# Layer norm at the end of a graph kernel: scaled sum and input joined on VectorE, deviation by square root and reciprocal

## The chip, the cores and the metric

The kernel runs on one core of a Trainium2 chip. The time is the device time of that core in microseconds (us), the median of several executions. A profile is one execution taken by the hardware profiler. It has its own time, and within that a span, from the first instruction to the last.

## The reference, cut to what matters

A graph layer computes a message for each of 200000 edges, sums the messages into 12500 nodes of 64 features (`agg`), and then normalises in two steps:

```
new_node = g3 * (agg - mean0(agg)) * rsqrt(var0(agg) + 1e-5) + bt3      # per feature, over all nodes
h        = x + (x + new_node)
out      = (h - mean(h)) / sqrt(var(h) + 1e-5)                          # per node, over its 64 features
```

The change touches only these last lines: the batch norm's scale and shift, the sum with `x` taken twice, and the layer norm over 64 features.

## The kernel before, in words

Features lie on partitions and nodes on columns. A tile of 128 partitions holds two halves of the nodes, 64 features each, so all of it is 128 x 6250. The last stage cuts that into `PARTS`: N = 13 parts, twelve of 500 columns and one of 250. Everything before it (the edge stages, some 2487 us of the span) is left as it is.

The order of the work is written out by hand, one program per engine, with semaphores between them. A wait is on a count, so that slot n % 4 of a buffer (S = 4) or n % 3 (V = 3) is used again only when part n - 4 or n - 3 is done with it.

First half of the stage. TensorE folds `agg` into `y_ps` (L983), VectorE takes the statistics of each part (`bn_stats`, L1040), and ScalarE copies it to `total` (L1012). Then comes a serial stretch of tiny instructions, `norm_coefficients` (L1067 on) with two products in `pair_sums`. It gives scale and shift of each feature in `bn3`. One of its instructions is a reciprocal of one column (L1091). Its root runs on ScalarE (L1014).

Between the halves, VectorE scales the 128 x 128 centring matrix by the feature's scale (`centre_t`, L1044). TensorE makes the centred shift (L992), and VectorE copies it to `shift` (L1046). GpSimd has built the block average `average`, `centre` = identity minus average, and `centre_x` = 2 * centre.

Second half, for each part n:

- TensorE puts `centre_x` times x and `centre_t` times total into one `y_ps` (L1001, L1002), and behind that `average` times the square of part n - 1 into `var_ps` (L997).
- ScalarE squares `y_ps` with the shift as bias (L1031), and makes the inverse deviation of part n - 1 by Ln (L1024) and Exp with scale -0.5 (L1026).
- GpSimd squares the inverse deviation (L972), VectorE multiplies by the variance (L1052), makes y by a multiplication with the inverse deviation (L1053), and turns the product into the factor of a Newton step (L1056). GpSimd multiplies y by it (L966).
- SyncE sends y to memory, one DMA a part (L947), when GpSimd is done with it.

GpSimd's order is: square of part n, then the last multiplication of part n - 1.

Of the kernel before, what the change touches and what calls it, by code (L numbers as in the profile page):

```python
# [17 lines left out]
P = 128  # L18
# [89 lines left out]
def build(nc, xt, x_nodes, src_t, src_r, dst_t, dst_r, dst_h, dst_hr, e_main, e_ragged,  # L108
          x, w_dst, w_src, w_edges, b1, g1, bt1, g2, bt2, g3, bt3, out):
    ctx = ExitStack()  # L110
    with ctx:
# [15 lines left out]
        def sem(name):  # L127
            return ctx.enter_context(nc.semaphore(name))
# [35 lines left out]
        with stage:  # L164
            def sb(name, shape, dt=F32):
                return stage.enter_context(nc.sbuf_tensor(name, shape, dt))
# [736 lines left out]
        with stage:  # L903
            def sb(name, shape, dt=F32):
# [7 lines left out]
            x_sb = sb("x_sb", [P, N_HALF])  # L912
            total = sb("total", [P, N_HALF])
            square = [sb(f"square{s}", [P, COLS]) for s in range(S)]
            inv_dev = [sb(f"inv_dev{s}", [P, COLS]) for s in range(S)]
            refine = [sb(f"refine{s}", [P, COLS]) for s in range(V)]
            eps = sb("eps", [P, 1])
            y = sb("y", [P, N_HALF])
            average = sb("average", [P, P])
            centre = sb("centre", [P, P])  # L920
            centre_x = sb("centre_x", [P, P])
            centre_t = sb("centre_t", [P, P])
            stats = sb("stats3", [P, N, 6])
            shift = sb("shift", [P, 1])
            y_ps = [stage.enter_context(nc.psum_tensor(f"y_ps{s}", [P, 512], F32)) for s in range(S)]
# [4 lines left out]
                sem(n) for n in ("x_in4", "folded", "f_copied", "f_counted", "aggr3", "paired3", "rooted3", "bn3_steps"))  # L930
            averages, centres, scaled, shift_summed, shift_set = (
                sem(n) for n in ("averages", "centres", "scaled", "shift_summed", "shift_set"))
            centred, squared, averaged, logged, inverted, inv_squared, multiplied, divided, refined, normed, stored = (
                sem(n) for n in ("centred", "squared", "averaged", "logged3", "inverted", "inv_squared", "multiplied",
                                 "divided", "refined", "normed", "stored"))

            def width(n):
                return PARTS[n].stop - PARTS[n].start
# [3 lines left out]
            @blk.sync  # L942
            def _(sp):
                sp.dma_start(x_sb[:], x_nodes).then_inc(x_in4, 16)
                for n in range(N):
                    sp.wait_ge(normed, n + 1)
                    sp.dma_start(out[:, PARTS[n]], y[:, PARTS[n]]).then_inc(stored, 16)  # L947
                sp.wait_ge(stored, 16 * N)

            @blk.gpsimd  # L950
            def _(gp):
                gp.memset(eps[:], EPS).then_inc(averages, 1)
                gp.memset(average[:], 0.0).then_inc(averages, 1)
                gp.wait_ge(averages, 2)
                for h in range(2):
                    lanes = slice(h * F, (h + 1) * F)
                    gp.memset(average[lanes, lanes], 1.0 / F).then_inc(averages, 1)
                gp.wait_ge(averages, 4)
                gp.tensor_tensor(centre[:], ident[:], average[:], ALU.subtract).then_inc(centres, 1)
                gp.wait_ge(centres, 1)  # L960
                gp.tensor_tensor(centre_x[:], centre[:], centre[:], ALU.add).then_inc(centres, 1)

                def finish(n):
                    gp.wait_ge(divided, n + 1)
                    gp.wait_ge(refined, n + 1)
                    gp.tensor_tensor(y[:, PARTS[n]], y[:, PARTS[n]], refine[n % V][:, 0:width(n)], ALU.mult).then_inc(normed, 1)  # L966

                for n in range(N):
                    part = inv_dev[n % S][:, 0:width(n)]
                    gp.wait_ge(inverted, n + 1)  # L970
                    after(gp, normed, n - V + 1)
                    gp.tensor_tensor(refine[n % V][:, 0:width(n)], part, part, ALU.mult).then_inc(inv_squared, 1)  # L972
                    if n > 0:
                        finish(n - 1)
                finish(N - 1)

            @blk.tensor
            def _(pe):
                for n in range(N):
                    after(pe, f_counted, n - S + 1)  # L980
                    after(pe, f_copied, n - S + 1)
                    for h in range(2):
                        mm = pe.matmul(y_ps[n % S][h * F:(h + 1) * F, 0:width(n)], fold[:, 0:F],  # L983
                                       agg[:, h * N_HALF + PARTS[n].start:h * N_HALF + PARTS[n].stop], start=True, stop=True)
                    mm.then_inc(folded, 1)
                pair_sums(pe, fold, tmp, pair_ps, aggr, paired)
                pe.wait_ge(x_in4, 16)
                pe.wait_ge(f_copied, N)
                pe.wait_ge(averages, 4)
                pe.wait_ge(centres, 2)  # L990
                pe.wait_ge(scaled, 1)
                pe.matmul(pair_ps[:, 2:3], centre[:], bn3[:, 1:2], start=True, stop=True).then_inc(shift_summed, 1)  # L992

                def variance(n):
                    pe.wait_ge(squared, n + 1)
                    after(pe, multiplied, n - V + 1)
                    pe.matmul(var_ps[n % V][:, 0:width(n)], average[:], square[n % S][:, 0:width(n)], start=True, stop=True).then_inc(averaged, 1)  # L997

                for n in range(N):
                    after(pe, divided, n - S + 1)  # L1000
                    pe.matmul(y_ps[n % S][:, 0:width(n)], centre_x[:], x_sb[:, PARTS[n]], start=True, stop=False)  # L1001
                    pe.matmul(y_ps[n % S][:, 0:width(n)], centre_t[:], total[:, PARTS[n]], start=False, stop=True).then_inc(centred, 1)  # L1002
                    if n > 0:
                        variance(n - 1)
                variance(N - 1)

            @blk.scalar
            def _(act):
                for n in range(N):
                    act.wait_ge(folded, n + 1)  # L1010
                    act.wait_ge(f_counted, n + 1)
                    act.activation(total[:, PARTS[n]], y_ps[n % S][:, 0:width(n)], ACT.Copy).then_inc(f_copied, 1)  # L1012
                act.wait_ge(aggr, 3)
                act.activation(tmp[:, 7:8], tmp[:, 6:7], ACT.Sqrt).then_inc(rooted, 1)  # L1014
                act.preload_act_table_set("natural_log_exp_and_others")
                act.wait_ge(averages, 4)
                act.wait_ge(shift_set, 1)

                def invert(n):

                    part = inv_dev[n % S][:, 0:width(n)]
                    act.wait_ge(averaged, n + 1)
                    after(act, divided, n - S + 1)
                    act.activation(part, var_ps[n % V][:, 0:width(n)], ACT.Ln, bias=eps[:]).then_inc(logged, 1)  # L1024
                    act.wait_ge(logged, n + 1)
                    act.activation(part, part, ACT.Exp, scale=-0.5).then_inc(inverted, 1)  # L1026

                for n in range(N):
                    act.wait_ge(centred, n + 1)
                    after(act, averaged, n - S + 1)  # L1030
                    act.activation(square[n % S][:, 0:width(n)], y_ps[n % S][:, 0:width(n)], ACT.Square, bias=shift[:]).then_inc(squared, 1)  # L1031
                    if n > 0:
                        invert(n - 1)
                invert(N - 1)

            @blk.vector
            def _(v):
                for n in range(N):
                    v.wait_ge(folded, n + 1)
                    v.bn_stats(stats[:, n, :], y_ps[n % S][:, 0:width(n)]).then_inc(f_counted, 1)  # L1040
                norm_coefficients(v, stats[:], f_counted, N, gb[:, 4:5], gb[:, 5:6], bn3,
                                  tmp, pair_ps, aggr, paired, rooted, bn3_steps)
                v.wait_ge(centres, 1)
                v.tensor_scalar(centre_t[:], centre[:], bn3[:, 0:1], None, ALU.mult).then_inc(scaled, 1)  # L1044
                v.wait_ge(shift_summed, 1)
                v.tensor_copy(shift[:], pair_ps[:, 2:3]).then_inc(shift_set, 1)  # L1046
                v.wait_ge(shift_set, 1)

                for n in range(N):
                    part = refine[n % V][:, 0:width(n)]  # L1050
                    v.wait_ge(inv_squared, n + 1)
                    v.scalar_tensor_tensor(part, var_ps[n % V][:, 0:width(n)], eps[:], part, ALU.add, ALU.mult).then_inc(multiplied, 1)  # L1052
                    v.scalar_tensor_tensor(y[:, PARTS[n]], y_ps[n % S][:, 0:width(n)], shift[:], inv_dev[n % S][:, 0:width(n)],  # L1053
                                           ALU.add, ALU.mult).then_inc(divided, 1)
                    v.wait_ge(multiplied, n + 1)
                    v.tensor_scalar(part, part, -0.5, 1.5, ALU.mult, ALU.add).then_inc(refined, 1)  # L1056


def pair_sums(pe, fold, tmp, pair, aggr, paired):
# [87 lines left out]
```

## Time and profile before

| what | us |
|---|---|
| median of 3 runs (2549.99 to 2551.42) | 2550.4 |
| the profiled execution's own time | 2551.55 |
| its span | 2549.6 |
| first half of the last stage and its coefficients, in the span | from 2487.4 |
| second half | from about 2506 |

The page's row of engines gives busy time over the whole span, most of which belongs to the edge stages. The stage of the change is the last fortieth of it, so the rows below are read from stretches of the trace near its end. Instants are microseconds from the span's start.

### The profile page before, as it was taken

What the parts mean: (1) busy time and instruction counts of PE and PEld (TensorE: products, weight loads), DVE (VectorE), ACT (ScalarE), POOL (GpSimd) and SP (SyncE); (2) the same over time, 40 slices, a digit from 0 to 9 for tenths busy, and PEclk for the clock granted to TensorE, in tenths of its full rate; (3) what the DMA queues carried; (4) which work ended last, traced back from release to release, by engine and by line L of the source; (5) the groups of instructions that cost most, each with busy time, mean ns of one, the idle gap of its engine ahead of it and who ended that gap; (6) DMA issues with size and microseconds to landing.
All of it is one profiled execution on the core that took longest, in us unless ns stands there. A gap on an engine that the chain in (4) does not pass through costs nothing. (4 is left out here: it accounts for less than half of the span.)

```text
span 2549.6 us, 31587 instructions
## 1 busy us (share of the span) xinstructions
PE 1829.1 (72%) x7288; PEld 775.3 (30%) x7288; DVE 1008.4 (40%) x1958; ACT 688.7 (27%) x724; POOL 1745.7 (68%) x1679
## 2 busy tenths in 40 slices
PE   5987778777878777787777787877777005776667
PEld 3322222222222222222222222222222004665553
DVE  4322222222222222222222222222223897887785
ACT  0111111111111111111111111111111978998835
POOL 7777777777777777777777777777775106666624
PEclk7766666666666666666666666666666558999998
DMA  7433333333333333333333333333345895876522
GB/s 210 118 92 99 92 98 91 93 97 90 97 94 90 101 91 95 96 90 98 93 92 99 90 94 97 94 96 91 94 126 192 302 353 198 257 248 215 190 83 101
DMA packets 247313, 327.52 MB, mean 128 GB/s; under 512 B 78146, under 2 KB 130762, under 8 KB 246957
## 3 DMA queue, kind: packets, MB, share of 16 engines
q1 hardware_dynamic: 167961, 220.98, 26.6%
q0 software_dynamic: 50048, 51.30, 10.4%
q10 hardware_dynamic: 29232, 54.42, 5.8%
q8 instruction: 27, 0.44, 0.1%
q14 instruction: 45, 0.37, 0.0%
HBM read 234.57 MB, written 91.96 MB: 128 GB/s over the span
## 5 line engine op out<-in xcount | busy, mean ns | idle before, releaser
L331 POOL DMA_INDIRECT rows<-x,idx x1564 | 1478.5, 945 | 480.6 <-issue 475.6
L536 DVE BATCH_NORM_STATS2 stats<-z_sb 128x512 f32 (+1 forms) x196 | 135.7, 692 | 1004.6 <-ACT z_sb L431 1004.6
L376 PE MATMUL xg_ps<-ident,rows 128*128 128x128 f32 (+1 forms) x782 | 213.5, 427 | 417.0 <-DMA rows<-x,idx 416.9
L370 PE MATMUL d_ps<-d_two,ones 1*84 1x512 f32 (+1 forms) x784 | 403.8, 636 | 11.3 <-DMA d_two<-dst_f 11.3
L380 PE MATMUL z_ps<-e_in,w_edge 96*128 96x512 f32 x392 | 373.3, 1056 | 0.0
L425 ACT ACTIVATE xg<-xg_ps 128x512 f32<-128x512 f32 x196 | 116.7, 596 | 899.8 <-PE xg_ps L376 899.8
L389 PE MATMUL z_ps<-xg,w_rows 128*128 128x512 f32 x392 | 346.0, 983 | 0.2 <-ACT xg L425 0.2
L431 ACT ACTIVATE z_sb<-z_ps 128x512 f32<-128x512 f32 x196 | 116.7, 596 | 799.7 <-PE z_ps L384 799.7
L376 PEld LDWEIGHTS xg_ps<-ident,rows 128*128 128x128 f32 (+1 forms) x782 | 136.2, 212 | 595.9 <-DMA rows<-x,idx 428.5
L759 POOL TENSOR_TENSOR h_buf<-h_buf,s_all 128x1536 f32<-128x1536 f32 x66 | 223.4, 3417 | 110.0 <-ACT h_buf L733 110.0
L519 DVE TENSOR_SCALAR hot<-d_ps,node_col 84x512 f32<-84x512 f32 x392 | 274.5, 740 | 41.2 <-PE d_ps L370 30.6
L384 PE MATMUL z_ps<-hot,q_in 84*64 84x512 f32 (+1 forms) x784 | 278.9, 799 | 0.5 <-DVE hot L519 0.5
L770 PE MATMUL sum_ps<-near,h_rows 128*64 128x84 f32 x3128 | 158.7, 244 | 97.4 <-DVE agg L822 90.6
L370 PEld LDWEIGHTS d_ps<-d_two,ones 1*84 1x84 f32 x784 | 105.6, 154 | 344.0 <-issue 332.5
L389 PEld LDWEIGHTS z_ps<-xg,w_rows 128*128 128x128 f32 x392 | 123.9, 316 | 209.5 <-ACT xg L425 111.6
L450 DVE COPY idx<-src_idx 128x8 int32 (+1 forms) x195 | 35.3, 182 | 364.0 <-PE xg_ps L376 358.1
L770 PEld LDWEIGHTS sum_ps<-near,h_rows 128*64 128x64 f32 x3128 | 131.2, 139 | 128.1 <-issue 103.8
L830 DVE COPY h_rows<-turn_ps 128x512 f32<-128x512 f32 x196 | 129.3, 687 | 17.3 <-PE turn_ps L780 7.0
L384 PEld LDWEIGHTS z_ps<-hot,q_in 84*64 84x64 f32 x784 | 49.9, 176 | 266.2 <-issue 266.2
L629 DVE BATCH_NORM_STATS2 stats<-s_all 128x512 f32 (+1 forms) x195 | 116.9, 677 | 6.0 <-ACT s_all L612 5.4
L822 DVE TENSOR_TENSOR agg<-agg,sum_ps 64x84 f32 x392 | 93.4, 238 | 51.7 <-issue 42.9
L745 ACT ACTIVATE h_buf<-s_all,bn 128x1536 f32<-128x1536 f32 x66 | 108.3, 1641 | 20.0 <-PE turn_ps L780 19.7
(122 smaller groups left out, 1056.8 us busy)
## 6 DMA issues: line engine op xcount, KB each, us to landing
s_all<-edge_mem SPq DMA_DIRECT2D x118, 768.0 KB, 6.5
edge_mem<-z_sb ACTq DMA_DIRECT2D x195, 256.0 KB, 2.1
e_in<-e_main SPq DMA_DIRECT2D x195, 192.0 KB
near_mem<-near_one SPq DMA_DIRECT2D x195, 168.0 KB, 2.0
near<-near_mem SPq DMA_DIRECT2D x65, 504.0 KB, 3.8
rows<-x,idx POOLq DMA_INDIRECT x1564, 2.5
q_in<-q_table SPq DMA_DIRECT2D x392, 21.0 KB
agg<-xt SPq DMA_DIRECT2D x7, 448.0 KB, 10.7
```

The source lines that it names most:

```text
L331: gp.indirect_dma_start(out=rows[s][0:size.tile, t, h, :], out_offset=None, in_=x, in_offset=bass.IndirectOffsetOnAxis(ap=idx[s][0:size.ti ...
L370: mm = pe.matmul(d_ps[0:WIN, h, 0:w], ones[s % 2 * F:s % 2 * F + 1, 0:WIN], d_in[s][:, h, 0:w], start=True, stop=True)
L376: mm = pe.transpose(xg_ps[s % 2][:, t * size.tile:(t + 1) * size.tile], rows[s][0:size.tile, t, :, :].rearrange("p h f -> p (h f)"), ident ...
L380: pe.matmul(z_ps[s % 2][:, 0:w], w_edge[:], e_in[s][:, 0:w], start=True, stop=False)
L384: mm = pe.matmul(z_ps[s % 2][h * F:(h + 1) * F, 0:w], which(h), hot[:, h, 0:w], start=False, stop=last)
L389: pe.matmul(z_ps[s % 2][:, 0:w], w_rows[:], xg[s % 2][:, 0:w], start=False, stop=False)
L519: hots = v.tensor_scalar(hot[:, h, 0:size.half], d_ps[0:WIN, h, 0:size.half], node_col[0:WIN, bass.ds(g * 2 + h, 1)], None, ALU.is_equal)
L536: v.bn_stats(stats[:, bass.ds(g, 1), :].rearrange("p a k -> p (a k)"), z_sb[s][:, 0:size.half]).then_inc(z_counted, 1)
L629: ins = v.bn_stats(stats[:, bass.ds(c * CHUNK + k, 1), :].rearrange("p a k -> p (a k)"), s_in[s][:, k, :])
L759: gp.tensor_tensor(m.cols(h_buf[m.slot % H]), m.cols(h_buf[m.slot % H]), m.cols(s_in[m.slot]), ALU.mult).then_inc(h_ready, 1)
L770: mm = pe.matmul(sum_ps[k][h * F:(h + 1) * F, 0:WIN], h_rows[m.slot % 2][0:n.tile, k, t, h * F:(h + 1) * F], hots[0:n.tile, h * n.tiles + ...
L830: v.tensor_copy(h_rows[m.slot % 2][:, k][at], turn_of(m, k)[at]).then_inc(rows_ready, 1)
```

## The change

The two products into `y_ps` become one. VectorE now joins each part beforehand: total = total * (scale / 2) + x (`join`). Everything is thus at half the size of before, and the epsilon is a quarter to match. `centre_t` and `centre_x` are gone. The shift is halved in the instruction that took it out of PSUM.

The deviation is a square root on ScalarE, then a `reciprocal` on VectorE over the whole part, in place. Ln, Exp, GpSimd's square, the two VectorE instructions of the Newton step and GpSimd's multiplication are gone. GpSimd has nothing left to do in the second half. The table of the square root is loaded at the start of the stage and stays. The output DMA waits for VectorE.

VectorE's order: join of parts 0, 1, 2, then for each n: reciprocal of n, join of n + 3, y of n. All waits on `x` are VectorE's now.

```diff
-                gp.memset(eps[:], EPS).then_inc(averages, 1)
+                gp.memset(eps[:], EPS / 4).then_inc(averages, 1)
...
-                gp.wait_ge(centres, 1)
-                gp.tensor_tensor(centre_x[:], centre[:], centre[:], ALU.add).then_inc(centres, 1)
-
-                def finish(n):
-                    gp.wait_ge(divided, n + 1)
-                    gp.wait_ge(refined, n + 1)
-                    gp.tensor_tensor(y[:, PARTS[n]], y[:, PARTS[n]], refine[n % V][:, 0:width(n)], ALU.mult).then_inc(normed, 1)
-
-                for n in range(N):
-                    part = inv_dev[n % S][:, 0:width(n)]
-                    gp.wait_ge(inverted, n + 1)
-                    after(gp, normed, n - V + 1)
-                    gp.tensor_tensor(refine[n % V][:, 0:width(n)], part, part, ALU.mult).then_inc(inv_squared, 1)
-                    if n > 0:
-                        finish(n - 1)
-                finish(N - 1)
...
+                pe.wait_ge(f_copied, N)
                 for n in range(N):
+                    pe.wait_ge(joined, n + 1)
                     after(pe, divided, n - S + 1)
-                    pe.matmul(y_ps[n % S][:, 0:width(n)], centre_x[:], x_sb[:, PARTS[n]], start=True, stop=False)
-                    pe.matmul(y_ps[n % S][:, 0:width(n)], centre_t[:], total[:, PARTS[n]], start=False, stop=True).then_inc(centred, 1)
+                    pe.matmul(y_ps[n % S][:, 0:width(n)], centre[:], total[:, PARTS[n]], start=True, stop=True).then_inc(centred, 1)
...
             def _(act):
+                act.preload_act_table_set("sqrt_and_others")
...
-                act.preload_act_table_set("natural_log_exp_and_others")
...
-                def invert(n):
-
-                    part = inv_dev[n % S][:, 0:width(n)]
+                def deviation(n):
                     act.wait_ge(averaged, n + 1)
                     after(act, divided, n - S + 1)
-                    act.activation(part, var_ps[n % V][:, 0:width(n)], ACT.Ln, bias=eps[:]).then_inc(logged, 1)
-                    act.wait_ge(logged, n + 1)
-                    act.activation(part, part, ACT.Exp, scale=-0.5).then_inc(inverted, 1)
+                    act.activation(dev[n % S][:, 0:width(n)], var_ps[n % V][:, 0:width(n)], ACT.Sqrt, bias=eps[:]).then_inc(rooted_dev, 1)
...
-                v.wait_ge(centres, 1)
-                v.tensor_scalar(centre_t[:], centre[:], bn3[:, 0:1], None, ALU.mult).then_inc(scaled, 1)
+                v.tensor_scalar(half_scale[:], bn3[:, 0:1], 0.5, None, ALU.mult).then_inc(scaled, 1)
                 v.wait_ge(shift_summed, 1)
-                v.tensor_copy(shift[:], pair_ps[:, 2:3]).then_inc(shift_set, 1)
+                v.tensor_scalar(shift[:], pair_ps[:, 2:3], 0.5, None, ALU.mult).then_inc(shift_set, 1)
                 v.wait_ge(shift_set, 1)
-
+                v.wait_ge(scaled, 1)
+                v.wait_ge(x_in4, 16)
+
+                def join(n):
+
+
+                    v.wait_ge(f_copied, n + 1)
+                    v.scalar_tensor_tensor(total[:, PARTS[n]], total[:, PARTS[n]], half_scale[:], x_sb[:, PARTS[n]],
+                                           ALU.mult, ALU.add).then_inc(joined, 1)
+
+                for n in range(V):
+                    join(n)
                 for n in range(N):
-                    part = refine[n % V][:, 0:width(n)]
-                    v.wait_ge(inv_squared, n + 1)
-                    v.scalar_tensor_tensor(part, var_ps[n % V][:, 0:width(n)], eps[:], part, ALU.add, ALU.mult).then_inc(multiplied, 1)
-                    v.scalar_tensor_tensor(y[:, PARTS[n]], y_ps[n % S][:, 0:width(n)], shift[:], inv_dev[n % S][:, 0:width(n)],
-                                           ALU.add, ALU.mult).then_inc(divided, 1)
-                    v.wait_ge(multiplied, n + 1)
-                    v.tensor_scalar(part, part, -0.5, 1.5, ALU.mult, ALU.add).then_inc(refined, 1)
+                    v.wait_ge(rooted_dev, n + 1)
+                    part = dev[n % S][:, 0:width(n)]
+                    v.reciprocal(part, part).then_inc(inverted, 1)
+                    if n + V < N:
+                        join(n + V)
+                    v.wait_ge(inverted, n + 1)
+                    v.scalar_tensor_tensor(y[:, PARTS[n]], y_ps[n % S][:, 0:width(n)], shift[:], part, ALU.add, ALU.mult).then_inc(divided, 1)
```

## Rows read from the trace of the kernel before

**Rows 1.** The page: span, and engines' busy time over the whole span.
```profile
span 2549.6 us, 31587 instructions
PE 1829.1 (72%) x7288; PEld 775.3 (30%) x7288; DVE 1008.4 (40%) x1958; ACT 688.7 (27%) x724; POOL 1745.7 (68%) x1679
```

**Rows 2.** Busy time of each engine, coefficients, start, loop and tail of the stage.
```profile
core 0: us, PE busy (x) PEld busy (x) DVE busy (x) ACT busy (x) POOL busy (x), PEclk, DMA share, GB/s
2502.00:2506.00 4.00, 1.28 (x6) 1.14 (x6) 1.72 (x10) 2.84 (x4) 0.00 (x0) 0.63 0.00 0
2506.00:2511.00 5.00, 5.00 (x9) 2.32 (x9) 0.16 (x1) 0.68 (x1) 0.00 (x0) 0.61 0.01 2
2511.00:2547.20 36.20, 28.94 (x72) 13.22 (x70) 25.31 (x39) 24.14 (x38) 29.27 (x26) 0.96 0.21 80
```

**Rows 3.** Chain of waits, start and one loop turn: start, duration, engine, tile, line.
```profile
2508.13 1.67 PE y_ps L1002 x2
...
2522.86 1.24 POOL y L966
2524.09 1.17 POOL refine L972
2525.28 0.74 DVE refine L1052
2526.02 0.65 DVE y L1053
2526.67 1.08 DVE refine L1056
...
2527.89 1.24 POOL y L966
```

**Rows 4.** Groups by line and shape, 2470 to 2550: busy us, mean ns of one.
```profile
L966 POOL TENSOR_TENSOR y<-y,refine 128x500 f32<-128x500 f32 x12 | 14.9, 1245 | 2.1 <-DVE refine L1056 2.1
L997 PE MATMUL var_ps<-square,average 128*128 128x500 f32 x24 | 12.0, 582 | 0.0
L1053 DVE SCALAR_TENSOR_TENSOR y<-y_ps,shift,inv_dev 128x500 f32<-128x500 f32 x12 | 8.7, 727 | 0.0
L1053 DVE SCALAR_TENSOR_TENSOR y<-y_ps,shift,inv_dev 128x250 f32<-128x250 f32 x1 | 0.5, 469 | 0.0
L1031 ACT ACTIVATE square<-y_ps,shift 128x500 f32<-128x500 f32 x12 | 8.1, 677 | 8.7 <-PE y_ps L1002 8.7
L1024 ACT ACTIVATE inv_dev<-var_ps,eps 128x500 f32<-128x500 f32 x12 | 8.1, 677 | 1.8 <-PE var_ps L997 1.8
```

**Rows 5.** VectorE and TensorE in order of time, in the loop.
```profile
2518.97 1.00 PE L997 MATMUL var_ps<-square,average 128*128 128x500 f32 x2
2519.80 1.00 PE L1001 MATMUL y_ps<-x_sb,centre_x 128*128 128x500 f32 x2
2527.66 0.73 DVE L1052 SCALAR_TENSOR_TENSOR refine<-var_ps,eps,refine 128x500 f32<-128x500 f32 x1
2528.31 0.72 DVE L1053 SCALAR_TENSOR_TENSOR y<-y_ps,shift,inv_dev 128x500 f32<-128x500 f32 x1
2528.95 0.45 DVE L1056 TENSOR_SCALAR refine<-refine 128x500 f32<-128x500 f32 x1
```

**Rows 6.** Single lines of VectorE: count, duration ns min/median/max, first and last start.
```profile
L1091 DVE RECIPROCAL tmp<-tmp x3: 164/165/165, 1981.0 to 2504.5; 128x1 f32<-128x1 f32 x3
L1092 DVE TENSOR_TENSOR bn<-tmp,gb x3: 159/159/159, 1981.2 to 2504.7; 128x1 f32<-128x1 f32 x3
L641 DVE TENSOR_SCALAR high<-high x1: 153/153/153, 2114.3 to 2114.3; 128x1 f32<-128x1 f32 x1
L812 DVE TENSOR_TENSOR near<-iota_ps,rel x65: 1198/1208/1209, 2117.4 to 2473.1; 128x1008 f32<-128x1008 f32 x65
```

**Rows 7.** In order of time, from the coefficients into the loop, and the last instruction.
```profile
2505.26 0.28 DVE L1044 TENSOR_SCALAR centre_t<-centre,bn 128x128 f32<-128x128 f32 x1
2505.69 0.56 PE L992 MATMUL pair_ps<-bn,centre 128*128 128x1 f32 x2 [1.73 <-DVE centre_t L1044]
2506.29 0.16 DVE L1046 COPY shift<-pair_ps 128x1 f32<-128x1 f32 x1 [0.74 <-PE pair_ps L992]
...
2546.41 0.71 POOL L966 TENSOR_TENSOR y<-y,refine 128x250 f32<-128x250 f32 x1 [0.29 <-DVE refine L1056]
```

**Rows 8.** Table loads, the load of x, and the last copies to total.
```profile
L1014 ACT ACT_TABLE_LOAD x1 | 1.3, 1283 | 0.0
L1015 ACT ACT_TABLE_LOAD x1 | 1.3, 1283 | 0.0
x_sb<-x_nodes SPq DMA_DIRECT2D x1, 3125.0 KB, 10.6
2487.39 0.34 SPq L944 DMA_DIRECT2D x_sb<-x_nodes  x1
2501.21 0.86 ACT L1012 ACTIVATE total<-y_ps 128x500 f32<-128x500 f32 x2 [0.25 <-DVE stats L1040]
```

More of the change, by code:

```diff
@@ L914, in build @@
             square = [sb(f"square{s}", [P, COLS]) for s in range(S)]
-            inv_dev = [sb(f"inv_dev{s}", [P, COLS]) for s in range(S)]
-            refine = [sb(f"refine{s}", [P, COLS]) for s in range(V)]
+            dev = [sb(f"dev{s}", [P, COLS]) for s in range(S)]
             eps = sb("eps", [P, 1])
@@ L920, in build @@
             centre = sb("centre", [P, P])
-            centre_x = sb("centre_x", [P, P])
-            centre_t = sb("centre_t", [P, P])
+            half_scale = sb("half_scale", [P, 1])
             stats = sb("stats3", [P, N, 6])
@@ L932, in build @@
                 sem(n) for n in ("averages", "centres", "scaled", "shift_summed", "shift_set"))
-            centred, squared, averaged, logged, inverted, inv_squared, multiplied, divided, refined, normed, stored = (
-                sem(n) for n in ("centred", "squared", "averaged", "logged3", "inverted", "inv_squared", "multiplied",
-                                 "divided", "refined", "normed", "stored"))
+            joined, centred, squared, averaged, rooted_dev, inverted, divided, stored = (
+                sem(n) for n in ("joined", "centred", "squared", "averaged", "rooted_dev", "inverted", "divided", "stored"))
             def width(n):
@@ L945, in _ @@
                 for n in range(N):
-                    sp.wait_ge(normed, n + 1)
+                    sp.wait_ge(divided, n + 1)
                     sp.dma_start(out[:, PARTS[n]], y[:, PARTS[n]]).then_inc(stored, 16)
@@ L986, in _ @@
                 pair_sums(pe, fold, tmp, pair_ps, aggr, paired)
-                pe.wait_ge(x_in4, 16)
-                pe.wait_ge(f_copied, N)
                 pe.wait_ge(averages, 4)
-                pe.wait_ge(centres, 2)
+                pe.wait_ge(centres, 1)
                 pe.wait_ge(scaled, 1)
@@ L995, in variance @@
                     pe.wait_ge(squared, n + 1)
-                    after(pe, multiplied, n - V + 1)
+                    after(pe, rooted_dev, n - V + 1)
                     pe.matmul(var_ps[n % V][:, 0:width(n)], average[:], square[n % S][:, 0:width(n)], start=True, stop=True).then_inc(averaged, 1)
+                pe.wait_ge(f_copied, N)
                 for n in range(N):
+                    pe.wait_ge(joined, n + 1)
                     after(pe, divided, n - S + 1)
-                    pe.matmul(y_ps[n % S][:, 0:width(n)], centre_x[:], x_sb[:, PARTS[n]], start=True, stop=False)
-                    pe.matmul(y_ps[n % S][:, 0:width(n)], centre_t[:], total[:, PARTS[n]], start=False, stop=True).then_inc(centred, 1)
+                    pe.matmul(y_ps[n % S][:, 0:width(n)], centre[:], total[:, PARTS[n]], start=True, stop=True).then_inc(centred, 1)
                     if n > 0:
@@ L1032, in _ @@
                     if n > 0:
-                        invert(n - 1)
-                invert(N - 1)
+                        deviation(n - 1)
+                deviation(N - 1)
             @blk.vector
```

## The prediction
> **What bounds the kernel now.** I read the page first: GpSimd and TensorE are busy for 68% and 72% of 2549.6 us [rows 1], but that is the edge stages, which the diff leaves alone. So I read the end of the span by stretches [rows 2]. The coefficients (2502 to 2506) are serial, with every engine mostly idle. In the next 5 us TensorE works without a gap at a granted clock of 0.61. Then the loop takes 36.2 us at 0.96, with GpSimd busy for 29.27 of it and TensorE for 28.94. VectorE has 25.31 and ScalarE 24.14.
>
> The chain of waits [rows 3] shows one turn: 5.03 us (2522.86 to 2527.89) between GpSimd's multiplications two parts apart, so 2.51 us a part, through GpSimd and VectorE in turn. TensorE is level with it. It starts one fp32 product of 500 columns each 0.83 us (2518.97, 2519.80) [rows 5], and three a part are 2.5 us. So the loop has two limits at about 2.5 us, and a part needs both shortened.
>
> **The change part by part.**
>
> *Removed.* Each part loses two instructions of GpSimd (L972, L966), two of VectorE (L1052, L1056), Exp on ScalarE, and one of three products on TensorE. What was 2.5 us on TensorE becomes 2 x 0.84 = 1.68 us. ScalarE keeps two instructions of 677 ns [rows 4], 1.36 us; I take the root at Ln's price, since Ln and Square, with the same operands, cost the same 677 ns. GpSimd has nothing to do. By these alone the loop would run at about 1.7 us a part. What is late next is VectorE.
>
> *VectorE, a part.* Three instructions: reciprocal, join, y.
>
> - y is L1053 as before: 727 ns for 500 columns, 469 ns for 250 [rows 4], so 1.03 ns a column. In a row of instructions each starts 0.65 us after the one in front (2527.66, 2528.31) [rows 5], 0.08 less than its duration. I take 0.65.
> - The join has the same form, but both tensors in SBUF. The nearest two-tensor row is 1208 ns for 1008 columns [rows 6], and 159 ns for one column. So 159 + 500 x 1.04 = 0.68 us, 0.60 from start to start. Bounds: 0.60 and 0.74, the latter the L1052 row in the chain. They move the sum by about 1.3 us.
> - The reciprocal of 500 columns does not occur in this trace. Only one of a single column does: 164 to 165 ns, where a two-tensor instruction of one column takes 159 and a scalar one 153 [rows 6]. One element lengthens the instruction by 5 to 6 ns over its neighbour. If all elements went through in a stream as in other instructions, one element should cost what theirs does. I therefore read the surplus as a price that each element pays: 1.03 + 5 to 1.03 + 6, that is 6.03 to 7.03 ns a column. I take the middle, 6.53: 500 x 6.53 + 160 = 3.42 us, and 1.79 us for 250 columns. Low end: a fixed surplus and 1.03 ns a column (or the 0.45 us of the scalar instruction L1056 [rows 5]). High end: the surplus over L641, 12 ns, paid by every column: 13.03 ns, 6.7 us.
>
> The Trainium skill, "VectorE: DVE Perf Modes", section "First, the fixed hardware budget", speaks against this change. It says that reciprocal is an iterated divide with a repeat count of 8 on two of the eight slices. The one-column surplus agrees in kind. Taken as eight passes of 1.03 ns it is the second rival below.
>
> *The loop.* With a join, a turn is (3.42 - 0.08) + 0.60 + 0.65 = 4.59 us. Joins run for n = 0 to 9, the last of them of 250 columns (0.34). Then: nine turns of 4.59 = 41.31; one of 4.33; two without a join, 3.42 + 0.03 + 0.65 = 4.10 each, 8.20 (y now waits for the reciprocal, with nothing between); the last 1.79 + 0.03 + 0.47 = 2.29. Sum 56.1 us.
>
> Does anything starve VectorE? The product of part n + 3 needs join n + 3, and the variance of n + 2 is queued behind it on TensorE. The root needed at the start of turn n + 1 hangs on join n + 2, which ended in turn n - 1, over 4 us earlier. Behind it are two products (0.84 each), a square and a root (0.68 each): 3.0 us. Even at the lower clock, where one product took 1.67 us of the chain [rows 3], TensorE needs 3.4 us a part, below 4.59. So neither TensorE nor ScalarE is seen, and the gap that TensorE now has costs nothing.
>
> *The start.* The 128 x 128 scaling (0.28) becomes a one-column instruction (0.16), so L992 starts 0.12 earlier, at 2505.57, and the shift is there at 2506.35 [rows 7]. New in the path is join 0, 0.68 us, to 2507.05, where before TensorE went straight on to x. Then at the lower clock two products of 1.67 (0 and 1, to about 2510.5), the variance of 0 (0.84 to 1.67), the root 0.15 + 0.68. The first reciprocal starts at 2512.2 to 2513.0; I take 2512.6. The joins of 1 and 2 lie beside product 0.
>
> *The new waits.* The joins wait for x, which landed 10.6 us after its issue at 2487.4 [rows 8], about 2498, so it is not late. The copies to `total` end at 2502.1 [rows 8]. The SyncE queue waits for y rather than for GpSimd's multiplication, and 250 KB every 4.6 us is less than it moved before. The two table loads of 1.28 us [rows 8] were already beside other work: the first ran in the wait for the coefficients, the second beside VectorE's last of them. Costed at 0 either way; uncovered they would give 1.3 us each.
>
> *The tail.* Before, the last instruction ended at 2546.41 + 0.71 = 2547.12, and the span 2.48 us later [rows 1, 7]. The last DMA is the same, so I keep that.
>
> *Sum.* 2512.6 + 56.1 + 2.5 = 2571.2, against a span of 2549.6: +21.6 us. On the profiled execution's own time that is 2551.55 + 21.6 = 2573.2. The median of the runs stands 1.15 under this, so I predict 2572.
>
> All 6250 columns pay, so the result moves by 6.25 us for each ns in the price of a column: the difference is 21.6 + 6.25 x (price - 6.53). It is zero at 3.07 ns. At 6.03 it is +18.5, at 7.03 +24.7.
>
> **The rivals.**
>
> 1. *Faster: the reciprocal streams.* At 1.03 ns a column a turn of VectorE is 0.60 + 0.60 + 0.65 = 1.85 us, still above TensorE's 1.68, and the difference is 21.6 - 6.25 x 5.5 = -12.8: 2537.6. It decides below 3.07 ns, 1.7 us for 500 columns. For it: VectorE's other instructions all show near 1 ns a column or less, and the surplus of 6 ns may be the start of a longer pipe. Against: that surplus is nearly six times the price of a column, and it is the same in all three instances. 12%.
> 2. *Eight passes a column.* 8 x 1.03 = 8.24 ns, 4.28 us for 500 columns, +32.3: 2582.7. For it: a one-column row cannot tell well what part of the fixed time a reciprocal saves, as the 153 ns of L641 shows against 159. Against: eight passes would show 7.2 ns over the two-tensor row, where 5 to 6 are seen. 23%. At the far end, 13.03 ns, it would be 2612.6; 4%.
> 3. *The tables switch in the loop.* If Square did not lie in the root's set, two loads of 1.28 us a part would stand beside ScalarE's 1.36: 3.9 us a part. At my price it hides behind the 4.59 of VectorE, apart from one or two loads at the start, some 2.6 us: 2575. If the reciprocal streams, 13 x (3.9 - 1.85) would turn -12.8 into about +14: 2564. For it: the trace has no Sqrt of many columns, and Square was seen only behind the Ln table. 3%.
>
> The Trainium skill, "ScalarE: Activation LUTs", section "Table sets: the hidden batching unit", says that cheap functions lie in every set and that only the anchors switch. No row here shows Square under the root's table.
>
> **How the numbers follow.** Price of a column between 5.3 and 7.6 ns, the forecast: 58%, 2564 to 2579. Rival 1 12%, rival 2 and its far end 27%, rival 3 3%. The range 2565 to 2584 takes in eight passes and rival 3, and leaves out rival 1, the far end and the edges of the forecast. This kernel's measurement tells 0.2%, 5.1 us, from no change. Faster by more is rival 1 without prices between 2 and 4 ns: 11%. Within 0.2%: 2%. Slower: 87%.
>
> **What would show it.** The group of RECIPROCAL rows of 128x500: 3.4 us each, thirteen of them on the chain of waits, with VectorE busy without gaps from about 2512 to 2569, and TensorE and ScalarE waiting for it. y 0.73 and join 0.68 us. Two products of 0.84 us a part or, if the clock falls in TensorE's gaps, longer with no effect. No GpSimd and at most one table load in the stage. Reciprocal rows near 0.7 us would make the prediction wrong in sign, rows over 4 us in size; a chain that goes through TensorE or ScalarE in the loop would refute the step that nothing starves VectorE.

## The result, and the profile after

The changed kernel takes 2571.47 us (median of 4 runs, 2570.59 to 2572.41), the kernel before 2550.91 in the same comparison. The ratio is 1.0078, with a 95% interval of 1.0061 to 1.0096: slower by 20.6 us. The prediction said 2572, in a range of 2565 to 2584.

The edge stages are the same code in both, yet the profiled execution of after reached the last stage about 2 us later. So the parts are compared by the *stage*: from the start of the aggregation of the last statistics (2501.48 before, 2503.41 after) to the end of the span (2549.6, 2570.1). That is 48.1 us before and 66.7 after, +18.6. The other 1.9 us of the two spans lie ahead of the change, in code that both share. In the four kernels of the experiments that ran beside each other, the same code brought the stage's start anywhere from 2500.16 to 2503.03.

Busy time of each engine by stretch, after (columns as in [rows 2]), start and loop:

```profile
2506.00:2511.00 5.00, 2.38 (x5) 1.36 (x6) 3.08 (x10) 0.20 (x1) 0.00 (x0) 0.50 0.00 0
2511.00:2567.20 56.20, 30.81 (x51) 10.31 (x49) 53.06 (x35) 17.08 (x26) 0.00 (x0) 0.77 0.14 54
```

Against [rows 2], where four engines shared 36.2 us, VectorE alone is now busy for 53.06 of 56.2. GpSimd has nothing. TensorE's granted clock has fallen from 0.96 to 0.77, and its 30.81 us for two thirds of the products (28.94 us for all of them before) show the price, yet it ends far below VectorE.

The chain of waits after, from the first product to the end of one turn (start, duration, engine, tile, line), and the last turns. It answers to [rows 3]:

```profile
2508.29 0.75 DVE total L1030
...
2509.18 3.30 PE y_ps L982 x4
2512.48 0.85 PE var_ps L976 x2
...
2513.36 0.69 ACT dev L1002
...
2514.07 3.28 DVE dev L1038
2517.34 0.56 DVE total L1030
2517.90 0.65 DVE y L1042
2518.55 3.18 DVE dev L1038
...
2565.72 1.63 DVE dev L1038
```

In the loop the chain has only one engine. L1038 is the reciprocal, L1030 the join, L1042 y. The first turn is 2514.07 to 2518.55, and each is 4.39 us from there on. The groups by line and shape, which answer to [rows 4, 6]:

```profile
L1038 DVE RECIPROCAL dev<-dev 128x500 f32<-128x500 f32 x12 | 39.2, 3266 | 3.7 <-ACT dev L1002 3.7
L1038 DVE RECIPROCAL dev<-dev 128x250 f32<-128x250 f32 x1 | 1.7, 1707 | 0.0
L1042 DVE SCALAR_TENSOR_TENSOR y<-y_ps,shift,dev 128x500 f32<-128x500 f32 x12 | 8.8, 730 | 0.1
L1030 DVE SCALAR_TENSOR_TENSOR total<-total,half_scale,x_sb 128x500 f32<-128x500 f32 x12 | 7.8, 661 | 0.0
L982 PE MATMUL y_ps<-total,centre 128*128 128x500 f32 x24 | 17.3, 820 | 17.9 <-DVE total L1030 17.9
L1002 ACT ACTIVATE dev<-var_ps,eps 128x500 f32<-128x500 f32 x12 | 8.1, 677 | 6.5 <-PE var_ps L976 6.5
L989 ACT ACT_TABLE_LOAD x1 | 1.3, 1283 | 39.7 <-PEq L661 39.7
```

The two reciprocal shapes give (3266 - 1707) / 250 = 6.24 ns a column. The root costs what Ln did, 677 ns. One table load stands in the whole stage.

### The profile page after: what moved, and what is told of

It is laid out like the page before. It is cut to its first block and busy times, and to the rows that moved or that the text cites. A ratio compares the mean times of both kernels' runs of the same rounds, so it can differ in the third digit from the quotient of the medians.

```text
span 2570.1 us, 31480 instructions
## 1 busy us (share of the span) xinstructions
PE 1819.5 (71%) x7262; PEld 766.4 (30%) x7262; DVE 1038.5 (40%) x1958; ACT 679.6 (26%) x710; POOL 1717.4 (67%) x1652
## 5 line engine op out<-in xcount | busy, mean ns | idle before, releaser
L380 PE MATMUL z_ps<-e_in,w_edge 96*128 96x512 f32 x392 | 367.0, 1039 | 0.0
```

The lines of the kernel that those rows point to most:

```text
L380: pe.matmul(z_ps[s % 2][:, 0:w], w_edge[:], e_in[s][:, 0:w], start=True, stop=False)
```

## The experiments

There were ten runs, of nine kernels (e6 and e10 are the same one). Four shared one comparison, in which the kernel before took 2551.2 us. The other six ran in two comparisons, on two other chips, in which the kernel before itself took 3014 and 3034 us. There the edge stages were slower in every kernel. VectorE's part of the last stage was not: in `e7_sizes`, which holds the changed kernel whole, the reciprocal takes 3.27 us and the turn 4.39, as here. Across comparisons I therefore use the stage, and inside each its ratio. The 48.1 us of the kernel before were traced only where the edge stages were fast.

A stage is one execution, and TensorE's granted clock at its start is not the same in each. The same kernel gave 35.8 us in e6 and 33.9 in e10. In e6 the first products ran at 0.50, the lower of the two levels (1.2 GHz), and the first variance product took 1.67 us; in e10 the clock was back at 1.00 (2.4 GHz) by then and it took 0.85. So a difference of under 2 us between two stages says nothing until the start is taken out. All stages (e7 is left out, since its probes stand in the stage):

| kernel | stage us | time, and ratio to before [95%] |
|---|---|---|
| before | 48.1 | |
| changed | 66.7 | 2571.5, 1.0078 [1.0061, 1.0096] |
| e1_streamed | 38.1 | 2540.6, 0.9958 [0.9941, 0.9974] |
| e2_twice | 108.1 | 2611.9, 1.0238 [1.0221, 1.0255] |
| e3_join_alone | 58.2 | 2562.7, 1.0044 [1.0027, 1.0061] |
| e4_root_alone | 63.0 | 2565.6, 1.0060 [1.0043, 1.0077] |
| e6_lnexp | 35.8 | 2999.7 against 3014.4, 0.9945 [0.9923, 0.9966] |
| e8_streamed_ahead | 35.7 | 3020.4 against 3033.8, 0.9958 [0.9943, 0.9973] |
| e9_join_ahead | 51.6 | 3038.4 against 3033.8, 1.0008 [0.9991, 1.0024] |
| e10_lnexp_again | 33.9 | 3018.1 against 3033.8, 0.9947 [0.9928, 0.9966] |
| e11_changed_ahead | 66.5 | 3050.0 against 3033.8, 1.0054 [1.0031, 1.0077] |

**The reciprocal's price, taken away.**

```diff
-                    v.reciprocal(part, part).then_inc(inverted, 1)
+                    v.tensor_tensor(part, part, part, ALU.mult).then_inc(inverted, 1)
```

> The changed kernel with the reciprocal of each part replaced by a two-tensor multiplication of the same tile with itself. It leaves the reciprocal out, so y is multiplied by the variance and not divided by the deviation. Stage = from the start of bn_aggr to the end of the span: 48.1 us before (2549.6 - 2501.48), 66.7 us changed (2570.1 - 2503.41). Theory (the price of a column of the reciprocal is all that the change loses by; the rest of it gains): this instruction is 0.68 us, a turn of VectorE 0.60 + 0.56 + 0.65 = 1.81 us, the stage 66.7 - 12.5 x (3.19 - 0.60) = 34.3 us, the time about 2537. Rival (the join, its place ahead of the first product, or TensorE's lower clock cost as well): the stage stays above 40 us and TensorE or ScalarE stands on the chain of waits.

Stage 38.1 us, 28.6 less than the changed kernel and 10.0 less than before. So the rest of the change, taken together, gains, and the reciprocal turns that gain into the loss. But 34.3 was expected. The chain of waits of this run, two turns:

```profile
2514.54 0.68 DVE dev L1038
2515.22 0.66 DVE total L1030
...
2515.92 1.11 PE y_ps L982 x2
2517.03 0.85 PE var_ps L976 x2
...
2517.90 0.69 ACT dev L1002
...
2518.61 0.68 DVE dev L1038
```

From one VectorE instruction to the same one two parts later it is 4.07 us, so 2.04 a turn. Join n + 3 comes late in turn n, and through product, variance and root it holds up the instruction of part n + 2.

The theory on the price holds, and the missing 3.8 us have three sources. The first L1038 comes 11.84 us into the stage (2512.43) where the first reciprocal of the changed kernel came at 10.66, because the first products took 3.67 us and not 3.30, and the first variance product 1.67 and not 0.85: 1.2 us by TensorE's lower clock. The join takes 0.65 us from start to start here, where behind a reciprocal it takes 0.56: 0.9 us over ten joins. VectorE's own three instructions thus make 1.90 us a turn. From the first L1038 to the one of part 10 (2532.81) that is 18.7 us with the short last join, and it took 20.4: an estimate of 1.6 us for the late joins. So the latency is the smaller part, and VectorE was busy for 19.50 of these 20.38 us. The rival had part of it too: its clock was seen, and TensorE and ScalarE stand on the chain, but the stage is under its 40.

**The price doubled.**

```diff
+                    v.reciprocal(part, part).then_inc(once, 1)
+                    v.wait_ge(once, n + 1)
                     v.reciprocal(part, part).then_inc(inverted, 1)
```

> The changed kernel with the reciprocal of each part done twice, one behind the other, so the division becomes a multiplication by the deviation. Theory (every reciprocal is on the path): 12 x (3.27 + 0.03) + 1.71 + 0.03 = 41.3 us more, stage 108.0, time about 2613. Rival (part of the reciprocal lies beside work that the path would wait for anyway, as TensorE's products at the lower clock): less than 38 us more.

Stage 108.1, +41.4 against 41.3 worked out. Every reciprocal is on the path in full. TensorE's granted clock was 0.62 in the loop of this kernel, lower than in the changed one, and that cost nothing.

**The two halves of the change alone.** The kernel before with the join (its VectorE order: L1052, y, join of n + 3, L1056):

```diff
-                    pe.matmul(y_ps[n % S][:, 0:width(n)], centre_x[:], x_sb[:, PARTS[n]], start=True, stop=False)
-                    pe.matmul(y_ps[n % S][:, 0:width(n)], centre_t[:], total[:, PARTS[n]], start=False, stop=True).then_inc(centred, 1)
+                    pe.matmul(y_ps[n % S][:, 0:width(n)], centre[:], total[:, PARTS[n]], start=True, stop=True).then_inc(centred, 1)
...
+                    if n + V < N:
+                        join(n + V)
                     v.wait_ge(multiplied, n + 1)
```

> The kernel before with the join alone: one product per part, Ln, Exp and the Newton step kept. VectorE has four instructions a part: 0.65 + 0.65 + 0.56 and the 0.37 to 1.07 of L1056, so 2.2 to 2.9 us a turn; GpSimd 2.4 to 2.5; TensorE 1.68 at the full clock. Theory (the join takes TensorE off the path, but GpSimd and VectorE hold the turn at 2.5 us, and the start pays 0.75 us for join 0 less one product of 1.67): stage 47 to 50 us, time within 2 us of before. Rival (TensorE was the real limit before): a turn of 2.2 us, stage 44 us. Rival 2 (VectorE's fourth instruction lengthens the turn of VectorE and GpSimd to 2.9): stage 52.

All three were wrong: 58.2 us, 10 more than before. One stretch of its chain of waits:

```profile
2540.97 1.21 POOL refine L970
2542.20 0.74 DVE refine L1058
2542.94 0.65 DVE y L1059
2543.59 0.66 DVE total L1049
...
2544.29 1.11 PE y_ps L999 x2
2545.39 0.85 PE var_ps L993 x2
2546.27 0.69 ACT inv_dev L1021
2546.98 0.63 ACT inv_dev L1023
...
2547.68 1.05 POOL refine L970
```

6.71 us for two parts, while VectorE, the busiest engine, was at work for only 30.0 of 47 us (2511 to 2558). In the kernel before, a product waited only for a free slot. Now it waits for a join that stands behind L1058 and y of the part three earlier, and so behind GpSimd's square of that part (L970).

That stretch ran at the full clock. Earlier, from 2514.45 to 2522.31 and on to 2531.35, two parts took 7.86 and 9.04 us. TensorE stood idle for over a third of that time, its granted clock was 0.78 and 0.67, and products of 1.67 us stood in the path. So did two joins of 0.98 and 1.49 us beside GpSimd's multiplications (0.73 otherwise). Against 6.71 these two pairs lost 3.5 us, an estimate of what the lower clock and the longer joins took. No run separates them.

The kernel before with root and reciprocal alone, both products kept:

```diff
+                    v.wait_ge(rooted_dev, n + 1)
+                    part = dev[n % S][:, 0:width(n)]
+                    v.reciprocal(part, part).then_inc(inverted, 1)
+                    v.wait_ge(inverted, n + 1)
+                    v.scalar_tensor_tensor(y[:, PARTS[n]], y_ps[n % S][:, 0:width(n)], shift[:], part, ALU.add, ALU.mult).then_inc(divided, 1)
```

> The kernel before with root and reciprocal alone: two products per part kept, no join. A turn of VectorE is 3.19 + 0.02 + 0.74 = 3.95 us, as in the last turns of the changed kernel, against 4.39. Theory (VectorE bounds; the join costs its 0.56 us a turn there): 10 turns x 0.43 = about 4 us less than the changed kernel, stage 62 to 63.5, time about 2567. Rival (three products a part at the lower clock, 5.0 us, become the limit since TensorE has gaps): stage 70 us or more, time about 2575.

Stage 63.0, as the theory had it, and turns of 3.96 us. TensorE kept a granted clock of 0.92 with its three products. So next to a reciprocal on VectorE the join costs 3.7 us and gives nothing: the product that it spares was already beside VectorE's work.

**The join earlier.** In three kernels the joins were put five parts ahead of y:

```diff
-                for n in range(V):
+                AHEAD = 5
+                for n in range(AHEAD):
                     join(n)
...
-                    if n + V < N:
-                        join(n + V)
+                    if n + AHEAD < N:
+                        join(n + AHEAD)
```

> The run with the reciprocal replaced by a multiplication (it leaves the reciprocal out, y is wrong by that), and with the joins five parts ahead of y where they were three. With three ahead its stage was 38.1 us (2538.7 - 2500.59), not 34.3, and two turns took 4.07 us by the chain: VectorE's instruction 0.68, join 0.66, TensorE 1.11 and 0.85, root 0.69, then VectorE again two parts on. Theory (the join three parts ahead, seen two parts later through product, variance and root, is the limit; it is a latency and not an engine's work): with five ahead the turn goes to VectorE's 1.86 or TensorE's 1.68, stage 35 to 37 us. Rival (TensorE's clock in its gaps): unchanged, 38 us.

Stage 35.7 (from 38.1), with the same late start as e1 (first L1039 11.85 us in). Its chain runs through TensorE without a gap, a turn in 1.68 us for the first parts and later in 1.89:

```profile
2993.94 0.84 PE y_ps L982 x2
2994.78 0.84 PE var_ps L976 x2
2995.61 0.84 PE y_ps L982 x2
```

The 1.89 us are VectorE's. From 2994.68 on it starts a part every 1.89 us, and it is busy for 12.00 of the 12 us from 2996 to 3008. Of the 2.4 us gained, two joins of 0.65 us that moved into VectorE's idle time before the first L1039 give 1.3. The shorter wait gives only the rest, about 1.1 us.

> The kernel before with the join alone, now with the joins five parts ahead. With three ahead its stage was 58.2 us (2561.2 - 2503.03) against 48.1 before: two turns took 6.7 us by the chain, GpSimd 1.03, VectorE 0.74 + 0.65 + 0.66, TensorE 1.11 + 0.85, ScalarE 0.69 + 0.63, GpSimd again. Theory (latency through the late join): the product of a part can start a turn earlier, as soon as its slot is free, and the turn falls to GpSimd's 2.4 to 2.5: stage 47 to 50 us, time within 2 us of before. Rival (the fourth VectorE instruction and the port shared with GpSimd): stays above 55.

Stage 51.6 (from 58.2). So 6.6 us of the 10 go. Besides the latency they hold what the lower clock cost in the loop (it is 1.00 here) and two joins of 0.65 us that moved ahead of the loop. But 47 to 50 was too low. From 3000.47 to 3024.67 the chain is VectorE's alone now:

```profile
3005.19 1.16 DVE refine L1065
3006.34 0.65 DVE refine L1059
3006.99 0.65 DVE y L1060
3007.64 0.65 DVE total L1049
```

Four instructions make 3.10 us, with L1065 (L1056 of before) at 1.16 of the chain in each of these turns, where before it took 1.08 in one turn [rows 3] and 0.45 in the next [rows 5]. So the rival had part of it: with a fourth instruction VectorE does not fit under 2.5 us.

> The changed kernel with the joins five parts ahead and nothing else. Theory (VectorE's work is the limit, and only joins moved into its idle time before the first reciprocal help): two joins of 0.56 us leave the loop, stage 66.7 - 1.1 = 65.6, time about 2570.4, hardly to be told from the changed kernel. Rival (the late join also delays the changed kernel): 3 us or more below it.

Stage 66.5, against 66.7 and the 65.6 of the theory. The turns are 4.39 us again, and from the first reciprocal to the end of the last y it is 52.9 us, 0.9 less than the 53.8 of the changed kernel, as the theory has it. The stage hides this, since the first reciprocal came 0.8 us later in it (11.44 against 10.66). The joins did not cause that, since they had ended 3.63 us before it. TensorE's lower clock did: the first products took 3.67 us and not 3.30, and the first variance product 1.68 and not 0.85. In the changed kernel the late join costs nothing, since its latency of 3.6 us (product 2517.95 to end of the root 2521.57 in the profile after) runs beside the reciprocals.

**The deviation without reciprocal and without Newton step**, on the changed kernel's join:

```diff
-                    act.activation(dev[n % S][:, 0:width(n)], var_ps[n % V][:, 0:width(n)], ACT.Sqrt, bias=eps[:]).then_inc(rooted_dev, 1)
+                    part = dev[n % S][:, 0:width(n)]
+                    act.activation(part, var_ps[n % V][:, 0:width(n)], ACT.Ln, bias=eps[:]).then_inc(rooted_dev, 1)
+                    act.wait_ge(rooted_dev, n + 1)
+                    act.activation(part, part, ACT.Exp, scale=-0.5).then_inc(inverted, 1)
...
-                    v.wait_ge(rooted_dev, n + 1)
-                    part = dev[n % S][:, 0:width(n)]
-                    v.reciprocal(part, part).then_inc(inverted, 1)
```

> The changed kernel with its join, but the inverse deviation made by Ln and Exp on ScalarE, with no reciprocal and no Newton step, so the last digits that the Newton step gave are left out. VectorE has join and y, 1.2 us a part; TensorE 1.68; ScalarE square, Ln and Exp, about 2.1 us with their issue gaps. Theory (without the 3.27 us instruction the next limit is ScalarE): a turn of 2.1 us, stage 39 to 41 us against 48.1 before and 66.7 changed, time 2542 to 2544, faster than both. Rival (TensorE's clock falls in its gaps and its two products take 3.3 us a part): stage above 52.

> The same kernel as e6_lnexp (join, Ln and Exp, no reciprocal, no Newton step, so its last digits are left out), timed again because the earlier runs, of the kernel before too, were some 450 us longer in the edge stages. Its stage there was 35.8 us (2998.4 - 2962.57) against 48.1 before. Theory: the stage is the same here, 35.8, and the time 12 us below before, about 2539. Rival: the gain there belonged to the edge stages, and here it is under 5 us.

Stages 35.8 and 33.9, and ratios of 0.9945 and 0.9947 whose intervals end below 1: faster than the kernel before, and by the stage than both. The second comparison also met slow edge stages, so the expected 2539 us was not seen as a time. The 12 to 14 us of gain are inside the stage. The chain of e10:

```profile
3005.65 0.66 ACT square L1011
3006.31 0.58 ACT dev L1004
3006.93 0.07 issue
3007.02 0.42 issue
3007.44 0.66 ACT square L1011
```

ScalarE is the limit, 1.79 us a turn for its three instructions, and busy for 4.90 of 5 us (3005.80 to 3010.80). The pieces called "issue" lie where Exp (L1006) runs. I had expected 2.1 and a stage of 39 to 41 us from the durations. But square, Ln and Exp, of 0.66, 0.67 and 0.62 us, start at 3005.65, 3006.21 and 3006.91, and the next square at 3007.44: two of the three start before the one in front has ended. No run has this kernel with both products kept, so what the join adds to this gain is not shown.

**The disputed cost by itself.** Behind the last y of the changed kernel, one at a time:

```diff
+                    with nc.allow_low_precision(reason="probe"):
+                        v.reciprocal(out_, ins_).then_inc(probed, 1)
...
+                for cols in (1, 250, 500):
+                    gp.tensor_tensor(pool_out[:, 0:cols], x_sb[:, 0:cols], power[:, 0:cols], ALU.pow).then_inc(pooled, 1)
```

> The changed kernel, and behind its last y, one at a time on VectorE: reciprocals of 128 partitions x 1, 8, 64, 250 and 500 columns, of 64 partitions x 500, of 500 columns of bf16, and of 500 columns from PSUM; then on GpSimd a two-tensor power of 1, 250 and 500 columns. Theory (six passes of the engine per column, 6.24 ns, and 148 ns fixed, whatever the type and the source): 154 to 165 ns, 198, 547, 1707, 3266, 3266, 3266 and about 3300 ns. Rival (the price is one of bytes or of the read port): bf16 takes half, or 64 partitions less. For the power no theory: below 2.2 us for 500 columns it could replace root and reciprocal.

Groups by line and shape of this run (busy us, mean ns of one):

```profile
L1070 DVE RECIPROCAL probe_out<-y_ps 128x500 f32<-128x500 f32 x1 | 3.3, 3283 | 0.0
L1070 DVE RECIPROCAL probe_out<-probe_in 128x500 f32<-128x500 f32 x1 | 3.3, 3278 | 0.0
L1070 DVE RECIPROCAL half_out<-half_in 128x500 bf16<-128x500 bf16 x1 | 3.3, 3277 | 0.0
L1070 DVE RECIPROCAL probe_out<-probe_in 64x500 f32<-64x500 f32 x1 | 3.3, 3270 | 0.0
L1070 DVE RECIPROCAL probe_out<-probe_in 128x8 f32<-128x8 f32 x1 | 0.2, 203 | 0.0
L1070 DVE RECIPROCAL probe_out<-probe_in 128x1 f32<-128x1 f32 x1 | 0.2, 164 | 0.0
L968 POOL TENSOR_TENSOR pool_out<-x_sb,power 128x250 f32<-128x250 f32 x1 | 40.3, 40313 | 0.1
L968 POOL TENSOR_TENSOR pool_out<-x_sb,power 128x500 f32<-128x500 f32 x1 | 80.2, 80242 | 0.1
```

6.25 ns a column ((3278 - 203) / 492), and the 500 columns take the same within 13 ns in fp32 and bf16, from PSUM and on half the partitions. So the price does not go by bytes, by source or by partitions, and the rival is refuted. It is six times the 1.03 ns of a column of y. The fixed part is 153 ns. GpSimd's power, at 80 us, is no way out.

## Why the prediction was right

**The bound.** "What is late next is VectorE": so it was, for 53.06 of 56.2 us.

**The price of a column.** Forecast 6.53 ns from one-column rows, bounds 6.03 and 7.03; measured 6.24 in the loop. Over 6250 columns the 0.29 ns are 1.8 us. The surplus of one column was a fair guide, but not by its reasoning alone, and with luck in the choice of neighbour: against the two-tensor row of 159 ns it gives 1.03 + 5 to 6, but the fixed part of the long reciprocals is 153 ns, that of L641, and from there the one-column row would have said 12. The first column costs some 5 ns more than the later ones do (164 ns, where 153 + 6.25 would be 159), which the prediction's reading of the surplus did not allow for.

**The loop.** 56.1 us forecast, 53.8 measured (2514.07 to 2567.85): 1.8 by the price, 0.4 by 0.56 in place of 0.60 for nine joins, since a join behind a reciprocal lasted 0.64 us (the first three, one behind another, some 0.73), and the rest by the fixed part, 147 ns in this kernel and not 160.

**The start and the tail.** The first reciprocal was due at 2512.6. It came at 2514.07, less the 1.93 by which the whole stage was late 2512.1. The forecast gave the first variance product 0.84 to 1.67 us by the clock, and it took 0.85. In e1 and e11 it took 1.67 and 1.68, so some 0.8 us of the start are chance. Tail 2.25 us (forecast 2.48).

**The sum.** By stage, 2571.2 - 2501.48 = 69.7 forecast and 66.7 measured: +21.6 against +18.6, every term a little too long. That the time came within 0.6 us of the forecast is luck to the extent of the 1.9 us that the edge stages took longer in after. One slip changed nothing: of the thirteen reciprocals that the forecast wanted at 128x500, twelve have that shape and the last is 128x250, as its own sum has it.

**The starvation step** was right at this price only. It compared four microseconds of lead with 3.0 us of work. At 6.25 ns a column the lead is there (e11: no gain from an earlier join). At streaming price it is not: TensorE and ScalarE stand on the chain of e1. Rival 1, worked out as -12.8 us, measured -10.0 in stage there, and an estimated 1.6 us of the difference are this wait; the later start and joins of 0.65 in place of 0.60 us are the rest. With the joins earlier (e8) it was -12.4, of which 1.3 are joins moved out of the loop. Its direction and its place were right; whether it would come about hung on the price alone, and 6.24 is twice the 3.07 from which it decides.

**Rival 1**, the streaming reciprocal, is refuted by the same rows: 3266 ns, where it wanted some 0.7 us. **Rival 2**, eight passes, is refuted too: 6.25 / 1.03 is six. The Trainium skill, "VectorE: DVE Perf Modes", section "First, the fixed hardware budget", gives a repeat count of 8 for the divide; the slope measured here is six columns' worth, and the measurement decides. That the count speaks against this change was borne out, its size was not.

**Rival 3**, table loads in the loop: the groups show one load in the stage and none in the loop, Square and Sqrt both at 677 ns. The Trainium skill, "ScalarE: Activation LUTs", section "Table sets: the hidden batching unit", says that cheap functions lie in every set. Square is not among its examples, and this trace bears the rule out for it.

**What the prediction did not see** is what its halves are worth. Join alone costs 10.0 us, root alone 14.9, both 18.6. The join is a cost where VectorE is the limit (e4 against the changed kernel: 3.7 us), and where it closes a loop of waits (e3). The kernels that gain (e6, e10) have the join and room on VectorE (12.94 of 18 us busy in e6), but that the join pays there is argued and not shown.

## What to carry to other kernels

A reciprocal costs VectorE six times as much a column as y does here, 3.27 us for 500 columns where the other two instructions of the turn take 0.64 and 0.73; count it before trading instructions on other engines for it, and if a trace holds only a one-column instance, bound its slope from its surplus over neighbours. A work item moved ahead of TensorE onto the engine that also finishes the parts adds a latency loop: count from that item to the instruction it finally releases, divide by the parts between, and move it further ahead if that is more than the busiest engine's turn. Before comparing two stages of single executions, take out what TensorE's clock did at their start. Ask of each half of a change what the other half's limit makes it worth.

## What the runs showed of the hardware

The reciprocal takes 6.25 ns a column from 8 to 500 columns of fp32 on 128 partitions, and 3270 to 3283 ns for 500 columns on 64 and on 128 partitions, in bf16 and fp32, from SBUF and PSUM (e7). GpSimd's two-tensor power takes 160 ns a column ((80242 - 40313) / 250). VectorE's scalar instruction of 500 columns (L1056 of before) took 1.16 us where a GpSimd multiplication had started just ahead of it (2521.41, then 2521.55), and 0.41 where it started together with one (2518.90, 2518.92), and then GpSimd's took 1.31 instead of 1.02. That the two take turns is read from these instants, and no run tests it. A join lasted 0.64 us behind a reciprocal, 0.73 in e1, and up to 1.49 in e3; why is open. The comparisons with edge stages over 450 us slower, in the kernel before as well, were on other chips than the fast one. Whether that is the cause was not looked into and stays open.
